# Second phase of a two-layer gated block: four buffers for probabilities, three for exponentials, and chunks transposed by halves

## What is computed

```python
x = x + tanh(g_xattn[0]) * fp8_product(layernorm(x), ctx)          # first phase
x = x + tanh(g_ffn[0])   * ternary_linear(int8(rms(layernorm(x)))) # from here on: second phase
x = x + tanh(g_xattn[1]) * attention(layernorm(x), ctx, ctx)       # 8 heads of 128 channels
x = x + tanh(g_ffn[1])   * top2_of_8_lora_experts(layernorm(x))    # router, Wa, Wb
```

## Time and profile before

| | us |
|---|---|
| median of 3 runs | 2032.5 (2029.92 to 2034.0) |
| profiled execution | 2032.83 |
| its span, first to last instruction | 2031.0 |
| PE busy | 1856.8 (91%) |
| DVE busy | 1542.6 (76%) |
| ACT busy | 1265.5 (62%) |
| POOL busy | 773.8 (38%) |
| share of 16 DMA engines, queue of SP | 79.6% |

### The profile page before, as it was taken

How to read it: one execution, slowest core, us unless ns; L and a number is a source line. 1 busy time by engine, 2 the same in 40 slices (tenths; PEclk the granted TensorE clock), 3 DMA queues, 4 the chain that set the end, 5 groups by cost and what they waited for, 6 DMA issues and landing times.

```text
span 2031.0 us, 26460 instructions
## 1 busy us (share of the span) xinstructions
PE 1856.8 (91%) x8968; PEld 838.4 (41%) x8968; DVE 1542.6 (76%) x2386; ACT 1265.5 (62%) x2045; POOL 773.8 (38%) x1100
## 2 busy tenths in 40 slices
PE   1699999894799999999999999999999999999997
PEld 0244444341344444444444444444444444444443
DVE  8899999888777777777777777777777777777662
ACT  4698898666556566656555565656565665555650
POOL 3555565333333333333333333333333333333320
PEclk9999999997999999999999999999999999999999
DMA  9687876796878888887788787888878878888772
GB/s 213 160 208 205 220 204 182 193 228 186 159 150 166 167 164 158 164 168 161 157 165 168 161 159 151 166 167 162 160 156 168 167 152 165 163 171 160 126 145 63
DMA packets 923975, 340.50 MB, mean 168 GB/s; under 512 B 849728, under 2 KB 898880, under 8 KB 923840
## 3 DMA queue, kind: packets, MB, share of 16 engines
q1 hardware_dynamic: 923840, 338.81, 79.6%
HBM read 93.36 MB, written 33.55 MB: 62 GB/s over the span
## 4 chain that ended last, share of the span: by engine, by line
DVE 21%; ACT 20%; issue 20%; POOL 10%; PE 7%; DMA 5%; SPq 0%; ACTq 0%; DVEq 0%; POOLq 0%
ACT slot L885 9%; DVE tiny L1586 7%; ACT arena L872 6%; POOL tiny L710 5%; DVE tiny L1220 4%; POOL tiny L708 4%; DVE slot L1591 3%; DMA probs<-slot 3%; ACT tiny L864 3%; DVE arena L1601 2%; ACT slot L909 2%; DVE slot L1559 2%; DMA slot<-slot 2%; DVE slot L1648 1%; DVE slot L1553 1%
## 5 line engine op out<-in xcount | busy, mean ns | idle before, releaser
L1591 DVE SCALAR_TENSOR_TENSOR slot<-arena,tiny,slot 128x1024 f16<-128x1024 f32 x256 | 328.2, 1282 | 306.0 <-ACT slot L885 305.9
L885 ACT ACTIVATE slot<-arena,tiny 128x1024 f16<-128x1024 f32 x256 | 293.6, 1147 | 174.1 <-POOL tiny L710 155.0
L1083 PE MATMUL sc<-arena,slot 128*128 128x512 f16 x1536 | 371.2, 382 | 19.2 <-ACT arena L872 17.0
L708 POOL TENSOR_SCALAR tiny<-tiny 128x1 f32<-128x1 f32 x256 | 100.1, 391 | 689.8 <-ACT arena L872 689.8
L1586 DVE TENSOR_REDUCE tiny<-sc 128x1 f32<-128x1024 f32 x256 | 306.5, 1207 | 16.5 <-PE sc L1083 15.1
L872 ACT ACTIVATE arena<-sc,tiny,head_tab 128x1024 f32<-128x1024 f32 x256 | 308.1, 1204 | 8.6
L864 ACT ACTIVATE tiny<-tiny,head_tab 128x1 f32<-128x1 f32 x256 | 73.9, 289 | 338.1 <-DVE tiny L1586 338.0
L1083 PEld LDWEIGHTS sc<-arena,slot 128*128 128x128 f16 x1536 | 150.1, 98 | 204.8 <-ACT arena L872 19.5
L1104 PE MATMUL accs<-probs,arena 128*128 128x512 f16 x512 | 196.9, 385 | 23.3 <-issue 21.1
L1106 PE MATMUL accs<-probs,arena 128*128 128x512 f16 x512 | 196.8, 384 | 0.0
L1105 PE MATMUL accs<-probs,arena 128*128 128x512 f16 x512 | 196.6, 384 | 0.0
(11 more groups left out here) (214 smaller groups left out, 2900.9 us busy)
## 6 DMA issues: line engine op xcount, KB each, us to landing
arena<-in_x SPq DMA_DIRECT2D x32, 512.0 KB, 4.2
x_scratch<-arena SPq DMA_DIRECT2D x32, 512.0 KB, 3.7
slot<-x_scratch SPq DMA_DIRECT2D x32, 512.0 KB, 4.1
slot<-in_ctx SPq DMA_DIRECT2D x32, 512.0 KB, 4.5
out<-arena SPq DMA_DIRECT2D x31, 512.0 KB, 3.4
slot<-in_L_ffn_Wa SPq DMA_DIRECT2D x12, 512.0 KB, 5.0
slot<-in_L_ffn_Wb SPq DMA_DIRECT2D x9, 512.0 KB, 4.9
wb_hi<-in_ctx SPq DMA_DIRECT2D x64, 64.0 KB, 2.5
```

The source lines that it names most:

```text
L885: act.activation(high, full, ACT.Identity, scale=rinv[c % 4][:]).then_inc(s_ph.sem, 1)
L1083: mm = pe.matmul(sc[:, c % 2, h * HALF:(h + 1) * HALF], q[i][:, c * P:(c + 1) * P], k[j][:, h * HALF:(h + 1) * HALF], start=start, stop=stop)
L1591: dve.scalar_tensor_tensor(out=low, in0=full, scalar=rinv[c % 4][:], in1=high, op0=ALU.mult, op1=ALU.subtract).then_inc(s_pl.sem, 1)
```

## The change

From tile 1 on the probabilities get four buffers `both` (two new ones in `late`) and the exponentials three buffers `full` (the third in `late`); tile 0 keeps four. Each chunk is transposed by two DMAs, one for the high part, issued once `prob_high` is done, and one for the low part. The orders of all five engines in the second phase are written anew. The scratch for descriptors made by GpSimd is set to 4096 bytes, which leaves room for the new buffers.

```diff
+        late = [sb(f"late{i}", [P, D]) for i in range(3)]
...
-        P2, T42 = [slot[i][:].bitcast(F16) for i in (12, 13)], slot[10][:].bitcast(F16)
+        P2 = [t[:].bitcast(F16) for t in (slot[12], slot[13], late[0], late[1])]
+        T42 = slot[10][:].bitcast(F16)
...
-        PF, X3 = (pf[:, 0], pf[:, 1]), (pf[:, 2], pf[:, 3])
-        PF_FIRST = PF + X3
+        PF, X3 = (pf[:, 0], pf[:, 1], late[2][:]), (pf[:, 2], pf[:, 3])
+        PF_FIRST = PF + X3[1:]
...
             if n == 0:
-                full, both = PF_FIRST[c % 4], P2_FIRST[c % 4]
+                full = PF_FIRST[c % 4]
             else:
-                full, both = PF[c % 2], P2[c % 2]
+                full = PF[(KB * n + c) % 3]
+            both = P2[c % 4]
...
             def turn_probs(n, c):
-                sp.wait_ge(s_ph.sem, s_ph.at(n, c + 1))
-                sp.wait_ge(s_pl.sem, s_pl.at(n, c + 1))
                 if c % 4 == 0:
                     after(sp, s_pv, n - 1, c // 4 + 1)
-                turned = s_pt_first[c % 4] if n == 0 else s_pt[c % 2]
-                sp.dma_start_transpose(PT[:, c // 4, :, (c % 4) * P:(c % 4 + 1) * P], chunk_buffers(n, c)[1])\
-                  .then_inc(turned.sem, 16)
+                for part, ready in enumerate((s_ph, s_pl)):
+                    sp.wait_ge(ready.sem, ready.at(n, c + 1))
+                    turned = PT[:, c // 4, part * KB:(part + 1) * KB, (c % 4) * P:(c % 4 + 1) * P]
+                    sp.dma_start_transpose(turned, chunk_buffers(n, c)[2 + part]).then_inc(s_pt[c % 4].sem, 16)
...
-                elif c >= 2:
-                    act.wait_ge(s_pl.sem, s_pl.at(n, c - 1))
+                elif n == 1 and c == 0:
+                    act.wait_ge(s_pl.sem, s_pl.at(0, KB - 1))
                 else:
-                    act.wait_ge(s_pl.sem, s_pl.at(n - 1, KB - 1 + c))
+                    act.wait_ge(s_pl.sem, s_pl.at(n, c - 2))
...
-                if n > 1 or n == 1 and c >= 2:
-                    act.wait_ge(chunks.sem, chunks.at(n - 1, 16 * (c // 2)))
+                if n > 0 or c >= 4:
+                    act.wait_ge(s_pt[c % 4].sem, s_pt[c % 4].at(n, 32 * (c // 4)))
...
-                if n == 0:
-                    dve.wait_ge(s_pl.sem, s_pl.at(0))
...
-    nc = _bacc.Bacc("TRN2", target_bir_lowering=False, num_devices=1)
+    nc = _bacc.Bacc("TRN2", target_bir_lowering=False, num_devices=1, dynamic_dma_scratch_size=4096)
```

## The result

The changed kernel takes 2039.45 us (median of 6 runs, 2038.52 to 2041.69) against 2031.21 for the kernel before in the same comparison: a ratio of 1.0042, 95% interval 1.0029 to 1.0054. It is slower, by 0.42% or some 8 us. The forecast was 2032 us, with more of the chance on faster than on slower. The profiled execution has a span of 2037.7 us, where that of before has 2031.0.

What follows compares the result with a forecast made beforehand. A chain of waits through DVE, ACT and POOL bounds each tile (47.22 us; TensorE alone 45.3). Steady tiles +8, ends -4.5, -2.3 and -1 give about 0 on the 2031.0 us span: 2032 us predicted, range 1998 to 2054.

Steps and rivals of the forecast that it cites:

- V: Zero of the forecast's times in a tile: the last matmul of the second values product, values(n-1,1), has been issued.
- step 2: POOL's ln_factors, held up by DVE's prob_low 0: L675 ends at V + 3.15, POOL done about 1.0 us late.
- 4: key_low ends / L710 of chunk 2 ends: DVE's prob_low 1 and key_low hold up POOL's row factor of chunk 2: V + 10.56, unhindered V + 9.0.
- 5: prob_high 2 starts / exp 4 ends: ACT starts prob_high 2 at V + 10.58; exp 4 follows 1.05 us later and ends at V + 13.25.
- 6: prob_low 2 ends / L708 of chunk 3 ends: POOL's query_low holds up DVE's prob_low 2, ending at V + 13.91; L708 of chunk 3 ends at V + 14.0.
- step 7: POOL's L710 of chunk 3 meets quantise_norm, V + 15.5; chunk 4's factor waits for quantise_scale, V + 16.7 to 16.9.
- 8: prob_high 4 starts / exp 5 ends: ACT's prob_high 4 at V + 16.8, exp 5 ended V + 19.4 to 19.5; scores 7 start V + 19.5 against 17.2.
- rival (d): Transposing transfers become the path if a half's fixed cost is serial: at least +67 us, 2100 us; chance 2%.
- Rival (c): L710 of chunk 3 misses the gap between quantise_norm and quantise_scale: 48.3 us a tile, +22, 2054 us; chance 17%.
- chain as laid out: Main case: POOL and DVE hold-ups meet as summed, 47.3 to 47.7 us a tile, 2026 to 2038 us; chance 45%.
- (a): POOL and DVE hold-ups don't meet as laid out: 46.0 to 47.1 us a tile, 1990 to 2021 us; chance 22%.
- (b): Hold-ups don't matter at all, TensorE is the bound: 45.3 to 45.6 us a tile, 1971 to 1980; chance 10%.

Runs made afterwards that it cites:

- The third, for step 2: Changed kernel with DVE's prob_low 0 moved behind row maxima 2 and 3: 2001.87 us, ratio 0.9848 to the kernel before.
- the one with both moves: Changed kernel with prob_low 0 behind maxima 2 and 3 and exp 5 ahead of prob_high 3 and 4: 1972.35 us, ratio 0.970.

## Why the prediction failed

**The mechanism was right.** Step by step, the same moments as forecast and in after (us from V):

| step | forecast | in after |
|---|---|---|
| 2: L675 ends | 3.15 | 3.13 |
| 3: rows_full starts | 4.18 | 4.16 |
| 4: key_low ends / L710 of chunk 2 ends | 10.13 / 10.56 | 10.13 / 10.57 |
| 5: prob_high 2 starts / exp 4 ends | 10.58 / 13.25 | 10.60 / 13.27 |
| 6: prob_low 2 ends / L708 of chunk 3 ends | 13.91 / 14.0 | 13.75 / 13.84 |
| 7: L710 of chunk 3 ends | 15.5 | 15.77 |
| 7: row factor of chunk 4 ends | 16.7 to 16.9 | 16.48 |
| 8: prob_high 4 starts / exp 5 ends | 16.8 / 19.5 | 16.86 / 19.51 |
| scores 7 start | 19.5 | 19.56 |

The wait ahead of values is gone, the holes ahead of scores 4, 5 and 7 are where they were put, no hole ends at a DMA, and two of the three experiments give back what their step holds: 1.26 us a tile for the 1.28 of L710 in step 7, 1.82 for the hole of 1.80 ahead of scores 7. The third, for step 2, gives 1.27 for 0.92, because later meetings shift too. Not all signs came true: the forecast had put L708 and L710 of chunks 2 to 4 near 1.0 us, and they took 0.94 and 1.46, 1.20 and 1.85, 0.47 and 0.58, so that the factor of chunk 4 was hardly held up. The argument against rival (d), that each half lands in 3.1 to 4.0 us, misreads: 4.0 is the median there, and the longest takes 6.9.

**Rival (c) half came true and cost nothing.** L710 of chunk 3 did miss the gap between quantise_norm and quantise_scale. But it ended 0.04 us behind quantise_scale, not 0.43, and its follower, released at once, was done at V + 16.48, so the 0.8 us that (c) had charged did not arise: prob_high 4 stands behind prob_high 3 on ACT (V + 15.81 + 1.05 = 16.86), which had room for it.

**What failed is a term of the sum, the +8 us of the 28 steady tiles, and the step "from there to the end", which had no term.** The first is a small difference of two nearly equal tile times. The forecast had a chain of 19.5 and 28.05 us, which is 47.55, wrote 47.5, subtracted 47.22, wrote 0.3 and took + 8 us. Unrounded, (47.55 - 47.22) x 28 = + 9.2; measured, 47.63, it is + 11.4. From the same marks as in the forecast, and with the start of the first scores product as one more:

| part of the span | forecast | measured |
|---|---|---|
| up to the first scores product | 0 | +1.2 |
| from there to the mark of tile 2 | -1 | -0.9 |
| 28 steady tiles | +8 | +11.4 |
| tile 30 to 31 | -4.5 | -4.1 |
| tile 31 to 32 | -2.3 | -2.5 |
| from there to the end | 0 | +1.5 |
| sum | 0 | +6.7 |

(Each measured line is rounded by itself; the sum is that of the spans.)

The first line can't be told from chance. The change rewrites the orders of the second phase only, and after's variants have the same first phase as after; yet the first scores product starts anywhere from 481.5 to 485.7 us in the traces of before, of after and of these variants. Timelines of TensorE, before and after:

```profile
481.58 0.59 PE L1083 MATMUL sc<-arena,slot 128*128 128x512 f16 x1 [2.21 <-ACT slot L905]
```

```profile
482.81 0.54 PE L1074 MATMUL sc<-arena,slot 128*128 128x512 f16 x1 [2.21 <-ACT slot L900]
```

The three terms behind it that the forecast did have, -1, -4.5 and -2.3, came out at -7.5 together instead of -7.8, but this was luck in part. The forecast subtracted from the times of before, and before has two stretches at the lower level of the clock (1.2 GHz), one in each of the last two second values products. In each, 8 matmuls start 0.43 us apart instead of 0.216, which costs 1.7 us. The view of before by windows (from, to, length, busy time and count of the five engines, then the granted clock, DMA share and GB/s):

```profile
1941.00:1948.40 7.40, 7.06 (x25) 2.87 (x26) 2.57 (x2) 3.16 (x5) 0.79 (x2) 0.77 0.74 143
1986.00:1993.00 7.00, 6.87 (x25) 2.78 (x26) 0.00 (x0) 0.00 (x0) 0.00 (x0) 0.76 0.00 0
```

In the 5 us ahead of 1941 TensorE was busy for 2.95, and ahead of the product at 1986.13 it had been idle for 2.13. After has no such stretch in these two steps, so 3.4 of the 7.5 us are clock, which the forecast hadn't seen and had taken at full speed without saying so; the version with one transfer for each chunk does have one.

The last term, from the last mark to the end, had been put at nothing without a word. Ahead of the last router TensorE waits 3.3 us for the turned rows in both kernels, and behind that wait it runs at the lower level: from 2009.88 to 2015.4 in after, 13 starts 0.43 us apart, where before has 6 of them. (13 - 6) x 0.21 = 1.5 us, which is the whole of the last line. This too may be chance and not the change: behind the same wait the version with exp 5 moved has 8 such starts, and the one with both moves 7. The timeline of TensorE in after, there:

```profile
2009.43 0.19 PE L1120 MATMUL accs<-rw_hl,slot 128*128 128x16 f16 x1 [3.30 <-DMA slot<-slot]
...
2010.26 0.63 PE L1055 MATMUL accs<-wa_both,slot 128*128 128x512 f16 x1
```

and from the view by windows, as above:

```profile
1998.20:2005.00 6.80, 6.80 (x33) 3.14 (x32) 3.60 (x5) 2.28 (x2) 2.16 (x7) 1.00 0.01 2
2005.00:2015.00 10.00, 6.70 (x35) 2.56 (x33) 3.32 (x16) 0.30 (x1) 0.00 (x0) 0.68 0.41 105
```

0.68, where the kernel before has 0.83 from 2000 to 2010.

**The chances.** The case "chain as laid out" had 45%, and it is what happened. But its band, 2026 to 2038, was drawn around a centre of 2032, which the terms above put too low: with all lines as measured it is 2039.5. So 12 of its 45 points stood on faster, though every tile of this chain is longer than 47.22 and only the ends could have made up for it. What cases (a) and (b), 32% together, asked for did not occur: no hold-up of steps 2, 4, 6 and 7 stayed out, and they do matter.

**Where the gain of the buffers and the halves went.** Each alone gives 0.4% on the old orders; the two weren't run together there. The new orders take away the wait ahead of values and the late transfers, and put a longer chain in their place: 47.63 us against the 46.85 of the earlier trace rows, + 0.78 a tile. Less than one hold-up decides this: prob_low 0 beside ln_factors is worth 1.27 us (47.63 - 46.36), the quantisation beside L710 1.26, and either move alone makes the change a gain of 1.4 to 1.5%. The two were not tried together. That it is the orders shows most directly in two versions that share buffers, scratch and whole transfers: 47.01 us a tile in the old orders (the kernel before with the buffers alone), 47.62 in the new ones (after with one transfer for each chunk). That the whole chain lies on the path at all is due to exp 5 behind prob_high 3 and 4.

The Trainium skill, SBUF — State Buffer, section "Who interferes with whom", says that a DVE instruction with at most one input in SBUF doesn't contend with GpSimd outside the two-port modes, and one with two does with a GpSimd instruction that reads SBUF. The runs agree at the place that matters: beside a maximum, which reads PSUM, L675 takes 0.19 us, and beside prob_low 0 it takes 1.11. L1433 (quantise_scale) has one input in SBUF, and yet L710 ended only with it; whether it ran in a two-port mode no run here shows.

## What to carry to other kernels

Where engines share a port, follow the small operations of the one beside the long ones of the other through the whole order, and again after every move: the hold-up that one operation leaves can be taken up by its neighbour, as when query_low was moved. Let the instruction that releases the bounding engine go ahead of work that has time, since this removed more (1.8 us a tile) than any single hold-up (1.3 us). And where a forecast is a difference of two tile times under 1% apart, keep every hundredth until the multiplication by the number of tiles, and give the ends and the first phase a range of their own: of the 6.7 us by which the span grew where the forecast had about 0, 3.4 lie in the steady tiles (0.12 us each), 1.5 behind the last mark and 1.2 in the first phase.

## What the runs showed that I had not expected

- A GpSimd operation of one column can be held up by two DVE instructions in a row: L710 took 1.85 us through L1427 and L1433 (1.27 and 0.75 us, 0.04 us apart), and 1.86 us in the version with query_low moved. Its end then is 0.04 to 0.05 us behind the second; behind key_low, whose follower was a maximum, the L710 of chunk 2 ended 0.44 us behind. It isn't always so: L708 of chunk 2 began beside prob_low 1 and ended at 1016.55, ahead of the end of key_low, which followed prob_low 1 at once. What decides isn't shown. The Trainium skill, SBUF — State Buffer, section "Who interferes with whom", has it that "Issue order, not op shape, decides who blocks". At this place the records don't show that order: L710 starts 1.06 us before L1433 and ends behind it. When it asked for the port is not to be seen, so this neither bears the sentence out nor refutes it.
- The hold-ups repeat to 0.01 us from tile to tile while no transfer lies on the path: 47.62 or 47.63 us in every steady tile, where the kernel before varies.
- hidden_low (L694), 1.16 us in all tiles of before, takes up to 1.75 us in after, beside an L1580; it has time there, and costs nothing.
- The same wait of 3.3 us at the end is followed by 6 slow starts in before, by 13 in after and by 7 or 8 in the versions named above. Why it differs stays open.
